# Expert part of a transformer kernel: layer norm of the mixed rows and the second input on VectorE instead of ScalarE and GpSimd, woven with the first output tile's mixing

## What is computed

```python
x = _layernorm(x + attention_layers(x))
h_norm = layer_norm(x, rn_g, rn_b)
g = softmax(h_norm @ router_w.T)
top2_w, top2_idx = top_k(g, 2)                  # weights of two experts
top2_w = top2_w / (sum(top2_w) + EPS_GATE)
hid = relu(layer_norm(x @ w1, ln_g, ln_b))      # per expert
expert_out = hid @ w2                           # per expert
out = sum(expert_out[top2_idx] * top2_w)        # the mixed rows
out = layer_norm(out, on_g, on_b)
x = _layernorm(x + out)
```

## Time and profile before

| what | value |
|---|---|
| median of 3 runs | 1008.57 us (1008.33 to 1008.92) |
| profiled execution | 1008.5 us, of which its span is 1006.7 us |
| first part | up to about 820 us |
| expert part | about 820 us to the end |

### The profile page before, as it was taken

How to read it: one execution, slowest core, us unless ns; L and a number is a source line. 1 busy time by engine, 2 the same in 40 slices (tenths; PEclk the granted TensorE clock), 3 DMA queues, 4 the chain that set the end, 5 groups by cost and what they waited for, 6 DMA issues and landing times.

```text
span 1006.7 us, 13398 instructions
## 1 busy us (share of the span) xinstructions
PE 954.6 (95%) x3604; PEld 607.4 (60%) x3604; DVE 888.4 (88%) x2338; ACT 825.6 (82%) x1341; POOL 99.2 (10%) x103
## 2 busy tenths in 40 slices
PE   8799999999999999999999999999999889999984
PEld 7455555555555555565555555555555567777773
DVE  6879999999999999999999999999998788888875
ACT  5889999999999999999899999999998854444442
POOL 2000000000000000000000000000001112333331
PEclk9999999999999999999999999999999999999997
DMA  9000000000000000020000000000001000000000
GB/s 342 1 1 0 1 1 1 0 1 1 0 1 1 1 0 1 1 85 0 1 1 7 0 1 1 1 0 1 1 0 62 23 1 1 11 11 12 12 21 21
DMA packets 8200, 15.86 MB, mean 16 GB/s; under 512 B 960, under 2 KB 5440, under 8 KB 8000
## 3 DMA queue, kind: packets, MB, share of 16 engines
q1 hardware_dynamic: 7696, 14.82, 4.2%
q10 hardware_dynamic: 432, 0.20, 0.1%
HBM read 12.92 MB, written 2.10 MB: 15 GB/s over the span
## 4 chain that ended last, share of the span: by engine, by line
PE 64%; ACT 15%; DVE 10%; issue 10%; POOL 1%; POOLq 0%; DVEq 0%; ACTq 0%
PE Oa L929 11%; PE Ob L929 7%; PE R L823 7%; PE R L825 6%; PE R L824 6%; PE SV L970 4%; ACT L668 4%; PE Ob L884 3%; ACT rs L510 2%; ACT L712 2%; ACT rz L489 2%; PE Ca L949 1%; PE Ca L948 1%; PE Cb L884 1%; PE SV L967 1%
## 5 line engine op out<-in xcount | busy, mean ns | idle before, releaser
L529 ACT ACTIVATE hid<-R,par 128x512 f32<-128x512 f32 x224 | 148.6, 698 | 14.2 <-PE R L825 12.2
L929 PE MATMUL Oa<-hid,wraw 128*128 128x512 f32 x256 | 134.6, 607 | 2.6 <-ACT hid L529 1.1
L929 PE MATMUL Ob<-hid,wraw 128*128 128x512 f32 x256 | 130.8, 592 | 0.0
L823 PE MATMUL R<-x_h,wf_h 128*128 128x512 f32 x224 | 106.1, 474 | 0.5 <-ACT hid L529 0.5
L510 ACT ACTIVATE rs<-SV,eps_ln 128x512 f32<-128x512 f32 x128 | 88.3, 690 | 10.1 <-PE SV L970 5.1
L1358 DVE SCALAR_TENSOR_TENSOR y<-x,par,y 128x512 f32<-128x512 f32 x120 | 87.4, 747 | 3.4 <-ACT y L538 3.1
L823 PE MATMUL R<-xr_h,wqkv_h 128*128 128x512 f32 x156 | 86.8, 556 | 2.5 <-DVE Kt L1314 1.1
L1369 DVE TENSOR_TENSOR y_l<-y,y_h 128x512 fp32r<-128x512 f32 x128 | 87.8, 686 | 1.2
L824 PE MATMUL R<-x_l,wf_h 128*128 128x512 f32 x224 | 88.0, 393 | 0.0
L825 PE MATMUL R<-x_h,wf_l 128*128 128x512 f32 x224 | 87.9, 392 | 0.0
L515 ACT ACTIVATE rs<-rs 128x512 f32<-128x512 f32 x128 | 80.7, 631 | 1.2
(11 more groups left out here) (274 smaller groups left out, 2413.4 us busy)
## 6 DMA issues: line engine op xcount, KB each, us to landing
wraw<-w_dram SPq DMA_DIRECT2D x7, 768.0 KB, 11.9
x<-x_dram SPq DMA_DIRECT2D x8, 256.0 KB, 6.0
Q<-x_dram SPq DMA_DIRECT2D x1, 2048.0 KB, 7.8
out_dram<-reluq SPq DMA_DIRECT2D x7, 256.0 KB, 2.3
wraw<-w_dram SPq DMA_DIRECT2D x2, 512.0 KB, 5.5
wraw<-w_dram SPq DMA_DIRECT2D x1, 576.0 KB, 6.4
wraw<-row_dram SPq DMA_DIRECT2D x1, 512.0 KB, 5.1
wraw<-bias_dram SPq DMA_DIRECT2D x1, 512.0 KB, 6.5
```

What stands on the lines that cost most here:

```text
L529: nc.scalar.activation(hid[:, m * CH:(m + 1) * CH], HIDDEN[m][:, :], GELU, bias=param(u // 4, BF1 + m % FB)).then_inc(hid_done, 1)
L823: nc.tensor.matmul(bank, w_h, a_h, start=True, stop=False)
L929: mm = nc.tensor.matmul(O[h][:, :], raw(u // 4, WF2 + j * P, P), hid[:, m * CH:(m + 1) * CH], start=(j == 0), stop=(j == FB - 1))
```

## The change

The mixed rows of an ending chunk are normed and added on VectorE. `norm_mix` on ScalarE (four instructions of 128 columns) goes. `scale_and_add` on GpSimd (two of 512 columns) goes. `negate_mean(MIX)` on VectorE goes too. In their place VectorE gets a `scale_and_add` of eight instructions of 128 columns: four compute (mixed - mean) * on_g, four that times rstd plus xb. It is woven as a third sequence with `mix_tile` 0 of chunk k - 1 and the four stages of the gating: after each mixing instruction and its gating stage comes one of the eight; the other four follow when the first two sequences have ended. The semaphore `mix_normed` goes, and `sum_done` now counts four for a chunk. The whole diff:

```diff
--- before.py
+++ after.py
@@ -270,7 +270,6 @@
         relu_done = sem("relu_done")
         expert_out_mm = sem("expert_out_mm")
         mix_done = sem("mix_done")
-        mix_normed = sem("mix_normed")
         mix_scaled = sem("mix_scaled")
         xb_done = sem("xb_done")
         sum_done = sem("sum_done")
@@ -583,16 +582,6 @@
                     act.wait_ge(wf2_mm, 2 * UNITS)
                 nc.scalar.activation(hid[:, m * CH:(m + 1) * CH], R[m % 3][:, :],
                                      ACT.Relu).then_inc(relu_done, 1)
-
-            def norm_mix(it, k):
-
-                n = upto_chunk(it, k)
-                act.wait_ge(rstd_done[1], n)
-                act.wait_ge(minus_mean_done[1], n)
-                for t in range(TILES):
-                    o = mix[:, par_tile(k, t)]
-                    nc.scalar.activation(o, o, ACT.Identity, bias=minus_mean[1][:, t:t + 1],
-                                         scale=rstd[1][:, t:t + 1]).then_inc(mix_normed, 1)
 
             def norm_sum(it, k):
 
@@ -783,8 +772,6 @@
                         relu(it, k - 1, m)
                     if (it, k) == (0, 1):
                         beside_first_chunk(m)
-                    if ends and m == 4:
-                        norm_mix(it, k - 2)
                     if enters and m == 6:
                         normalised(it, k + 1)
                 if routes:
@@ -1636,8 +1623,26 @@
                 dve.wait_ge(mix_done, upto_chunk(it, k) * TE)
                 yield from statistics(MIX, it, k, mix[:, half(k % 2)])
 
+            def scale_and_add(it, k):
+
+                n = upto_chunk(it, k)
+                dve.wait_ge(rstd_done[MIX], n)
+                dve.wait_ge(moments_step[MIX], n * MOMENT_STEPS)
+                for t in range(TILES):
+                    o = mix[:, par_tile(k, t)]
+                    nc.vector.scalar_tensor_tensor(out=o, in0=o, scalar=mean[MIX][:, t:t + 1], in1=on_g,
+                                                   op0=ALU.subtract, op1=ALU.mult).then_inc(mix_scaled, 1)
+                    yield
+                dve.wait_ge(xb_done, n)
+                for t in range(TILES):
+                    o = mix[:, par_tile(k, t)]
+                    dve.wait_ge(mix_scaled, (n - 1) * TILES + t + 1)
+                    nc.vector.scalar_tensor_tensor(out=o, in0=o, scalar=rstd[MIX][:, t:t + 1], in1=xb[:, par_tile(k, t)],
+                                                   op0=ALU.mult, op1=ALU.add).then_inc(sum_done, 1)
+                    yield
+
             def stats_sum(it, k):
-                dve.wait_ge(sum_done, upto_chunk(it, k))
+                dve.wait_ge(sum_done, upto_chunk(it, k) * TILES)
                 yield from statistics(SUM, it, k, mix[:, half(k % 2)])
 
             def negate_mean(which, it, k):
@@ -1834,8 +1839,6 @@
                     weave(first_gating, stats_z(it, k + 1))
                 else:
                     weave(squares(it, k, 1) if routes else none, stats_z(it, k + 1) if enters else none)
-                if ends:
-                    negate_mean(MIX, it, k - 2)
                 if first:
                     normalise(1, last, 0)
                     high(1, last, 0)
@@ -1850,7 +1853,8 @@
                     split_std(it, k)
                 if enters:
                     low_x(it, k + 1)
-                weave(mix_tile(it, k - 1, 0) if mixes else none, itertools.islice(gating, 4))
+                weave(mix_tile(it, k - 1, 0) if mixes else none, itertools.islice(gating, 4),
+                      scale_and_add(it, k - 2) if ends else none)
                 summing = stats_sum(it, k - 2) if ends else none
                 if first:
                     high_square(1, last, 1)
@@ -2053,20 +2057,10 @@
                 pool.wait_ge(x_var_done, 3 * upto_chunk(it, k))
                 nc.gpsimd.tensor_tensor(x_rstd[:, par_tiles(k)], x_var[:, par_tiles(k)], mhalf[:, 0:TILES], ALU.pow).then_inc(x_rstd_done, 1)
 
-            def scale_and_add(it, k):
-
-                n = upto_chunk(it, k)
-                o = mix[:, half(k % 2)]
-                pool.wait_ge(mix_normed, n * TILES)
-                nc.gpsimd.tensor_tensor(by_tile(o), by_tile(o), over_tiles(on_g, P), ALU.mult).then_inc(mix_scaled, 1)
-                pool.wait_ge(mix_scaled, n)
-                pool.wait_ge(xb_done, n)
-                nc.gpsimd.tensor_tensor(o, o, xb[:, half(k % 2)], ALU.add).then_inc(sum_done, 1)
-
             def add_on_b(it, k):
                 n = upto_chunk(it, k)
                 pool.wait_ge(xt_done, n * TILES)
-                after(pool, sum_done, n - 2)
+                after(pool, sum_done, (n - 2) * TILES)
                 nc.gpsimd.tensor_tensor(by_tile(xb[:, half(k % 2)]), by_tile(xt[:, half(k % 2)]),
                                         over_tiles(on_b, P), ALU.add).then_inc(xb_done, 1)
 
@@ -2084,8 +2078,6 @@
                 if enters:
                     to_minus_half(0, it, k + 1)
                     x_to_minus_half(it, k + 1)
-                if ends:
-                    scale_and_add(it, k - 2)
                 if ends:
                     to_minus_half(2, it, k - 2)
```

## The result

| | median | ratio to before, 95% interval |
|---|---|---|
| before | 1008.75 us (4 runs) | |
| the change | 1015.52 us (1014.45 to 1016.50, 4 runs) | 1.0072 [1.0058, 1.0086] |

Forecast were 1016.4 us (range 1011.5 to 1021.0) and slower by more than 0.2%. It came out 6.8 us slower. Of all executions in this document one, of the kernel with the eight before the gating, took 1175.84 us at a granted clock of 0.75; the ratios leave it out, the median of that kernel counts it.

The account below looks back on a forecast made before the run. The prediction took VectorE's queue from the gating to the next add_input as the chain; five steps gave + 5.5, (2, 3) + 1.4, (2, 4) + 1.0, so 1008.5 + 7.9 = 1016.4 us, range 1011.5 to 1021.0.

Parts of the forecast that it names:

- The stall: VectorE's 16-column sum in the gating, held beside GpSimd's two 512-column instructions: removing them gains 0.90 us in five steps.
- The eight: New VectorE instructions woven with mix_tile 0: 0.26 us each from start to start, 2.1 us a step.
- slack: VectorE's wait for TensorE before mix_tile 1, which the added work fills: 0.1 us in each of five steps.
- The bounds of 0.17 and 0.35: Least and most us for each new VectorE instruction: 1.4 or 2.8 us for eight; cheaper 0.09, dearer or stall stays 0.08.
- the rule of the Trainium skill: Two fp32 SBUF sources halve the new VectorE instructions' throughput: 0.13 us more each, 1023.9 us; chance 0.02.
- One step: Each of five steps, add_input to add_input: + 2.1 - 0.9 - 0.1 = + 1.1 us.
- the negated mean: negate_mean of the mixed rows leaving VectorE's squares: counted 0, hidden by waiting for gram products; at most 0.17 us gained.
- Steps (2, 3) and (2, 4): The two steps outside the usual five: + 1.4 us in (2, 3), + 1.0 us in (2, 4).
- The sum: All seven steps together: 5.5 + 1.4 + 1.0 = + 7.9 us, 1016.4 us.
- The range's cause: Price of each new VectorE instruction: 0.17 us gives 1011.5 us, 0.35 us gives 1021.3 us; stall staying gives 1020.9 us.
- What TensorE gives back: Turned deviations start up to 0.9 us earlier on TensorE, then lost waiting for mix_tile 1 and add_input.
- the eight run under expert_out 1: Faster rival: VectorE's new instructions fill a wait before mix_tile 1, 4.8 us less, 1003.7 us; chance 0.06.

Follow-up runs that it names:

- the kernel with the eight before the gating: The changed kernel with its eight instructions moved between squares 3 and the gating: 1007.28 us, ratio 0.9992 to before.
- both kernels that changed the pair alone: Changed kernel with GpSimd's two 512-column instructions added on an idle tile: 1019.82 us; kernel before with those two cut to 4 columns: 1003.91 us.
- four-of-eight kernel: The changed kernel without the first four of its eight instructions: 1008.83 us, ratio 0.9997 to before.
- three kernels: Changed kernel with the eight before the gating, 1007.28 us, or spread over VectorE's waits, 1003.85 us; two 512-column VectorE instructions before the gating instead, 1003.17 us.

## Why the prediction was right

**The stall.** Forecast 0.90 us a step. The sum went from 1.07 to 0.18 in the rows, the time between the gating's first instruction and mix_tile 0 from 3.69 to 2.80 us, and both kernels that changed the pair alone agree (0.75 and 0.8 a step). The step held.

**The eight.** Forecast 2.1 us, by 0.26 each. From mix_tile 0 to mix_tile 1 it is 3.93 us (905.95 to 909.88) where it was 1.98, + 1.95, which is 2.1 less a slack of nearly 0.15. The four-of-eight kernel gives 0.26 each again. The bounds of 0.17 and 0.35 were not needed. The instruction with both tensors in SBUF costs no second time for its columns, 0.26 from start to start for 128 of them; the rule of the Trainium skill that was weighed (Vector Engine (DVE) Microarchitecture Reference, Points that are easy to get wrong) would have given 1023.9 us and doesn't hold here.

**One step.** Forecast + 1.1, measured + 1.0: the slack was nearly 0.15 and not 0.1, and the negated mean that left the squares, which I counted at 0, gave 0.07 (10.69 to 10.62 us from add_input to the gating's first instruction). I had said that the squares behind it wait for TensorE's gram products; that was misread. Squares 2 started at 896.01, 0.08 behind L1646 and without a wait. Over five steps the slack and the mean are 0.6 us.

**Steps (2, 3) and (2, 4).** The timelines of VectorE, with expert_out 0 of step (2, 4) from TensorE's, answer to the earlier trace rows:

```profile
974.46 0.34 DVE L1614 TENSOR_SCALAR V<-Ob,rz 128x128 f32<-128x128 f32 x1
...
978.40 0.34 DVE L1614 TENSOR_SCALAR V<-Ca,rz 128x128 f32<-128x128 f32 x1
...
994.33 0.35 DVE L1614 TENSOR_SCALAR V<-Ob,rz 128x128 f32<-128x128 f32 x1 [8.02 <-PE Ob L1086]
...
997.47 0.35 DVE L1614 TENSOR_SCALAR V<-Ca,rz 128x128 f32<-128x128 f32 x1
...
992.23 2.05 PE L1086 MATMUL Ob<-wraw,hid 128*128 128x128 f32 x16 [0.69 <-ACT hid L583]
```

In (2, 3) mix_tile 1 starts 3.94 us behind mix_tile 0, before it was 2.57: + 1.4 as forecast. In (2, 4) it is 3.14 instead of 1.79, + 1.35, and the wait before expert_out 0 is 0.69 instead of 0.95, - 0.26; + 1.1, forecast + 1.0.

**The sum.** Forecast were + 7.9. With the measured sizes, + 0.97 in a usual step, it is 5 x 0.97 + 1.4 + 1.1 = 7.3 us, and 6.9 were measured in the rest. The last 0.4 is a single step before the change, (1, 3), which took 22.69 us where its neighbours took 22.33; I had counted all as 22.34. What made it longer is not known, so that part of the distance to the forecast is chance. The range's cause, an uncertain price of an instruction, was not what moved the time.

**What TensorE gives back.** Said was that it waits for mix_tile 1 and add_input. It does, 1.26 us before expert_out 3. That expert_out 2 begins about where it did was right too (5.63 us behind the gating's first instruction before, 5.53 after), but expert_out 1 ends earlier, so a wait of 0.79 us for mix_tile 0 opens, of which I said nothing. It had no part in the sum; that the wait is divided went with a clock that stayed up.

**The rivals.** That the eight run under expert_out 1 failed where it was said to: there is no wait of 2 us before mix_tile 1. Its idea was right for another place. VectorE waits 1.21 us before the gating, and work put there is free as far as the wait reaches, as three kernels show.

## What to carry to other kernels

Price an instruction added to the engine on the chain by the distance of starts, and look in that engine's own timeline for the wait that it could fill; where in the order the same eight instructions stood decided here between 0.7% slower and 0.5% faster. Look for small instructions that last many times their least duration: a 16-column sum of 1.07 us was worth more than the two 512-column instructions beside it. And before moving work between engines, ask which part of the change has the gain: here it was the end of the stall, and it can be had with two wide instructions in a wait.

## What was not expected of the hardware

VectorE's sum of two SBUF inputs doesn't run slower beside GpSimd's elementwise instruction of 512 columns in these rows, it ends when that one ends: 1.07 us for 16 columns, 0.93 beside a shorter one, with no data in common. Not every instruction is held. Three rows of VectorE in the kernel before, while L2070 ran on GpSimd until 895.17:

```profile
893.97 0.28 DVE L1511 SCALAR_TENSOR_TENSOR Kt<-Oa,x 128x128 f32<-128x128 f32 x1
...
894.17 0.30 DVE L1443 BATCH_NORM_STATS2 rz<-Cb 128x6 f32<-128x128 f32 x1
894.50 0.69 DVE L1449 TENSOR_TENSOR rz<-rz 128x4 f32<-128x4 f32 x1
```

The square with one input from PSUM (0.28) and the statistics of a PSUM tile (0.30) pass; the 4-column sum of two SBUF inputs lasts until 895.19. The changed kernel still has this one (0.70 us for 4 columns in step (0, 4), at 897.54); what it costs was not tried. And GpSimd's power of 4 columns holds nobody, as two rows of GpSimd and VectorE from the same execution show:

```profile
909.09 1.02 POOL L2049 TENSOR_TENSOR rz<-rz,mhalf 128x4 f32<-128x4 f32 x1 [7.63 <-DVE rz L1463]
...
909.57 0.17 DVE L1608 TENSOR_TENSOR rz<-rz 128x16 f32<-128x16 f32 x1
```

A product of two SBUF inputs takes its 0.17 us in the middle of it. That the 512-column instructions hold VectorE since both engines read SBUF is not shown; these rows tell only which pairs of instructions did and which did not.

TensorE's granted clock fell to half, with 0.6 to 1.6 us lost in an expert_out, behind a single wait of 2.05 to 2.22 us in one of five such steps and, in another execution, in four of five; behind 0.79 and 1.26 us with an expert_out between them it did not in any step of two executions.
